# Low rank products of two neighbouring FFN blocks, each on half of TensorE's rows

## What is computed

```python
def _bitlinear(x, w_latent):
    scale = clip(mean(abs(w_latent), axis=1, keepdims=True), 1e-05, None)
    tern = clip(round(w_latent / scale), -1.0, 1.0)
    w = w_latent + stop_gradient(tern - w_latent)
    return x @ (w * scale).T

h = _bitlinear(x, w_fc) + gate * (x @ v.T @ fast_b.T @ u.T)      # hidden 2048, rank 16
r = maximum(h, 0.0)
y = _bitlinear(r * r, w_proj)

x = x + xattn(layernorm(x), ctx, ctx)
x = x + ffn(layernorm(x))
```

## Time and profile before

| | before |
|---|---|
| median of three runs | 2806.88 us |
| span of the profiled execution | 2803.6 us |
| TensorE busy with matmuls | 2666.3 us (95%) |
| VectorE busy | 1688.5 us (60%) |
| ScalarE busy | 1111.7 us (40%) |
| GpSimd busy | 377.6 us (13%) |

### The profile page before, as it was taken

The page is one execution under the profiler, slowest core; times in us unless marked ns, Lnnn a source line. Parts: engine busy times, 40 slices in busy tenths (PEclk is TensorE's granted clock), DMA queues, the critical chain, the costliest instruction groups (busy, mean ns, idle before and its releaser), DMA issues. The chain is left out here.

```text
span 2803.6 us, 46166 instructions
## 1 busy us (share of the span) xinstructions
PE 2666.3 (95%) x15410; PEld 1979.3 (71%) x15410; DVE 1688.5 (60%) x3278; ACT 1111.7 (40%) x1965; POOL 377.6 (13%) x791
## 2 busy tenths in 40 slices
PE   7999999999999999999999967999999999999998
PEld 5666666667666666666766645888888888888887
DVE  4676766776767677677676666444444444444444
ACT  2533443443353344244335245444344334433332
POOL 1212121121121212112112110000000000000000
PEclk9999999999999999999999977999999999999999
DMA  4343253333334325333333332000000000000000
GB/s 129 84 112 99 61 135 92 81 98 98 88 85 114 97 62 134 90 79 103 98 85 88 96 104 76 30 30 30 30 30 30 30 30 30 30 30 30 30 30 31
DMA packets 116803, 198.81 MB, mean 71 GB/s; under 512 B 19987, under 2 KB 22035, under 8 KB 116260
## 3 DMA queue, kind: packets, MB, share of 16 engines
q1 hardware_dynamic: 116772, 198.42, 25.6%
HBM read 63.08 MB, written 33.55 MB: 34 GB/s over the span
## 5 line engine op out<-in xcount | busy, mean ns | idle before, releaser
L715 ACT ACTIVATE probs<-bank 128x512 f32<-128x512 f32 x640 | 369.2, 597 | 339.6 <-PE bank L529 329.6
L1125 PE MATMUL y_bank<-projT,a_hi 128*128 128x512 f32 x1024 | 409.1, 399 | 0.0
L1113 PE MATMUL h_bank<-x2T_hi,fcT 128*128 128x512 f32 x1024 | 406.2, 397 | 0.9 <-ACT scale_row L1196 0.9
L1114 PE MATMUL h_bank<-x2T_lo,fcT 128*128 128x512 f32 x1024 | 406.6, 397 | 0.0
L1127 PE MATMUL y_bank<-projT,a_lo 128*128 128x512 f32 x1024 | 403.9, 394 | 0.0
L1204 ACT ACTIVATE relu<-h_bank,scale_fc 128x512 f32<-128x512 f32 x256 | 176.0, 687 | 464.8 <-PE h_bank L1117 464.8
L464 POOL TENSOR_SCALAR_AFFINE_SELECT probs<-probs 128x256 f32<-128x256 f32 (+1 forms) x640 | 234.1, 366 | 872.7 <-ACT probs L715 870.1
L1314 DVE CAST a_hi<-act_sq 128x512 fp32r<-128x512 f32 x256 | 121.0, 472 | 373.6 <-ACT act_sq L1209 373.6
L529 PE MATMUL bank<-stack 98*128 98x512 f32 (+3 forms) x1024 | 286.0, 351 | 28.3 <-ACT probs L715 26.0
L504 PE MATMUL bank<-stack 96*128 96x512 f32 (+3 forms) x1024 | 266.0, 330 | 17.8 <-DVE maxima L777 11.8
L777 DVE TENSOR_REDUCE maxima<-bank 128x1 f32<-128x512 f32 x256 | 175.9, 687 | 162.2 <-PE bank L508 162.2
(11 more groups left out here) (182 smaller groups left out, 4623.9 us busy)
## 6 DMA issues: line engine op xcount, KB each, us to landing
stack<-stage SPq DMA_DIRECT2D x768, 128.0 KB, 2.3
x_in<-in_x_dram SPq DMA_DIRECT2D x16, 1024.0 KB, 5.3
x<-x_res SPq DMA_DIRECT2D x64, 256.0 KB, 2.4
x_in_sb<-x SPq DMA_DIRECT2D x16, 1024.0 KB, 5.6
out_dram<-y_sb SPq DMA_DIRECT2D x64, 256.0 KB, 2.0
xc_rows<-in_ctx_dram SPq DMA_DIRECT2D x15, 1024.0 KB, 5.2
stack<-m_stage SPq DMA_DIRECT2D x128, 8.0 KB, 1.8
w_nat<-in_L_ffn_w_fc_dram SPq DMA_DIRECT2D x2, 1024.0 KB, 6.7
```

The costliest lines, as they stand in the source:

```text
L715: act.activation(probs[:, s[2], :], t_bank[u % 2][:, :], ACT.Exp, scale=SCALE).then_inc(exp_done, 1)
L1113: pe.matmul(h_bank[b % 2][:, :], fcT[:, k, cols], xT_hi[:, k, :], start=k == 0, stop=False)
L1114: pe.matmul(h_bank[b % 2][:, :], fcT[:, k, cols], xT_lo[:, k, :], start=False, stop=False)
L1125: pe.matmul(y_bank[j][:, :], a_hi[:, b % RING, P * j:P * j + P], projT[:, b, :], start=b == 0, stop=False)
```

## The change

Each pair of blocks b - 1 and b (b odd) has its two low rank products issued one after the other behind the eight large matmuls of block b. The product of the even block takes rows 0 to 63 of `u_stack` and `z_sb`, that of the odd one rows 64 to 127; each writes its own bank and raises `h_full`. For this the four groups of 16 rows are packed into the first 64 rows (at 0, 16, 32 and 48), and stand a second time in the other 64: `a_stack` and `u_cols` are filled accordingly, and the low part of z is made in two operations of 16 rows. The wait for z moves from block 0 to block 1.

```diff
-    assert RANK <= 32 and D == 512 and KT == 4 and HIDDEN_LAG == KT
+    assert RANK == 16 and D == 512 and KT == 4 and HIDDEN_LAG == KT
...
+    HALF = P // 2
...
-                        if b == 0:
+                        if b == 1:
                             pe.wait_ge(xm_free, i * XJ + XJ)
-                        pe.matmul(h_bank[b % 2][:, :], u_stack[:, cols], z_sb[:, :], start=False, stop=True
-                                  ).then_inc(h_full, 1)
+                        if b % 2 == 1:
+                            for m in (b - 1, b):
+                                rows = slice(HALF * (m % 2), HALF * (m % 2) + HALF)
+                                pe.matmul(h_bank[m % 2][:, :], u_stack[rows, P * m:P * m + P], z_sb[rows, :],
+                                          start=False, stop=True).then_inc(h_full, 1)
...
-            for col in (0, 32, 64):
+            for col in (0, 16, 32, 64, 80, 96):
                 last = act.activation(a_stack[:, :, col:col + RANK], a_f32[:, :, :], ACT.Copy)
...
-                    dve.tensor_tensor(z_sb[32:64, :], x_bank[0][32:64, :], z_sb[32:64, :].bitcast(F32), ALU.subtract
-                                      ).then_inc(xm_free, 1)
+                    for at in (32, HALF + 32):
+                        last = dve.tensor_tensor(z_sb[at:at + RANK, :], x_bank[0][at:at + RANK, :],
+                                                 z_sb[at:at + RANK, :].bitcast(F32), ALU.subtract)
+                    last.then_inc(xm_free, 1)
...
-            dve.tensor_tensor(a_stack[:, :, 96:96 + RANK], a_f32[:, :, :], a_stack[:, :, 0:RANK].bitcast(F32),
-                              ALU.subtract).then_inc(prep, 1)
+            for col in (48, 112):
+                last = dve.tensor_tensor(a_stack[:, :, col:col + RANK], a_f32[:, :, :],
+                                         a_stack[:, :, 0:RANK].bitcast(F32), ALU.subtract)
+            last.then_inc(prep, 1)
...
-                    for col, src in ((0, u_hi), (32, u_hi), (64, u_lo), (96, u_hi)):
-                        last = dve.tensor_copy(u_cols[:, :, col:col + RANK], src[:, :, :].bitcast(F32))
+                    for odd in range(2):
+                        for col, src in ((0, u_hi), (16, u_lo), (32, u_hi), (48, u_hi)):
+                            at = HALF * odd + col
+                            last = dve.tensor_copy(u_cols[:, odd::2, at:at + RANK], src[:, odd::2, :].bitcast(F32))
```

## The result

The changed kernel takes 2854.5 us (median of four runs, 2851.3 to 2856.2) against 2806.9 us: a ratio of 1.0168, 95% interval 1.0153 to 1.0182. The forecast was 2857.3 us, in a range from 2834 to 2880, and slower. The profiled execution spans 2849.6 us, 46.0 more than the 2803.6 of before; the forecast for it was 50.4.

The account below looks back on a forecast made before the run. TensorE was taken to bound the FFN, every matmul slot counting. Terms +16.3, +32.6 and +1.5 gave +50.4 us, the span going from 2803.6 to 2854.0; with 3.3 for the median, 2857.3 us, range 2834 to 2880.

Parts of the forecast that it names:

- term 1: FFN pairs: TensorE empties around each, costing 0.17 us instead of saving 0.227; 96 pairs, +16.3 us.
- Rival (a): FFN pairs: no emptying for 64-row halves, loads hide under the last full matmul; 2812.8 us, chance 0.09.
- the assumption behind the 0.44: Within a pair: both halves' loads run together, so the halves start at 0.43 and 0.44 us.
- (b): Within a pair: the two loads follow one another, second half 0.107 us later; +10.3 us, 2867.6, chance 0.10.
- (c): Within a pair: halves run one after the other; 2879.1 us with emptying (chance 0.07), 2834.6 without (0.05).
- (e): FFN pairs: halves stream quicker than a full matmul, without emptying; 2797 us at half a slot, chance 0.03.
- term 2: Batch start: TensorE waits for relu before H2 and H4, +1.02 us each, 32 waits, +32.6 us.
- third wait: Batch start, H3 waiting for relu of block 1: forecast as hidden, relu ending at 2.94 and H2 at 3.59.
- rival (d): Batch starts: the clock falls, up to 1.7 us lost in each of 16 spells, +27; 2884 us, chance 0.05.
- term 3: Setup, run once: added copies, subtraction and z operation lengthen the chain, +1.5 us, between bounds 0 and 2.3.

Follow-up runs that it names:

- pairs_four_banks: Changed kernel with the blocks of h rotating through four PSUM banks instead of two, pairs kept; 2829.6 us.
- half_per_block: Changed kernel, but each block has its own 64-row half product behind its own eight matmuls, no pairs; 2910.4 us.
- quads_four_banks: Changed kernel with four banks, full products except blocks 4 to 11, whose half products stand four at a time behind blocks 7 and 11; 2806.7 us.
- both_on_lower_half: Changed kernel, but the odd block's product also lies on rows 0 to 63, so a pair can't run side by side; 2877.2 us.
- full_deferred: Changed kernel, but both products behind the odd block take all 128 rows instead of halves; 2835.7 us.
- layout_only: Changed kernel's filling and two z operations only; every block has its full product behind its own matmuls, z awaited at block 0; 2814.5 us.

## Why the prediction was right

- *The pair* (term 1) was put at 0.17 us, from the 0.07 at three borders in attention. Measured: 0.165 in pairs_four_banks. The step that carried the sign was to read those borders, of one-row and 128x32 products, as ones of any change of partition; half_per_block shows it for 64 rows, and the 0.07 came back as 0.07 and 0.08. Rival (a), in which the pairs would have saved 21.8 us and only the waits cost, falls with it. The Trainium skill's page "TensorEngine Tiling (Array Packing)", Key Properties, says that a change of tiling mode drains the engine, and the traces here agree: the loads come 0.33 and 0.43 behind the start of the matmul before them, where elsewhere they start with it. The Trainium skill's page "TensorE: Matmul & The Clock Gate", Step-by-step, lets a weight load be pulled ahead of running matmuls into the background buffer; the traces here show that inside one partition only, as with the second pair in quads_four_banks (its loads at 2020.46), and at no change of partition. From how few rows on a product counts as another partition no run settles: 96 rows keep the cover, 64 do not.
- *Both halves together*, the assumption behind the 0.44, held: both start in the same hundredth, and both_on_lower_half prices the other way at 1.37 per batch, or 0.23 for each of the six pairs that no wait follows. Rivals (b) and (c) fall. So does (e): in half_per_block a single half with its load exposed lasts 0.49 and the full matmul behind it, its load exposed too, 0.50; and the second pair in quads_four_banks lasts 0.40 like any full one. Halves stream no quicker.
- *The new waits* (term 2) were put at 1.02 each, two in a batch. Measured: 1.02 at the first pair, 0.85 more than a pair without wait (the changed kernel less pairs_four_banks: 0.85; the wait alone, in full_deferred: 0.84). Two such pairs and six at 0.165 make the 3.03 of a batch. The chain behind them came out step by step: half product to relu 0.42 after the exposed 0.11, relu 0.69, 0.05 to the load. There was no third wait.
- *The clock*: the granted clock is 1.00 over a batch (first line), and 1.00 at a batch start around the first new wait (second line), so rival (d) falls too:

```profile
2060.00:2125.00 65.00, 63.45 (x276) 1.00 0.09 32
2007.00:2010.00 3.00, 2.22 (x10) 1.00 0.22 87
```

  Only the very first matmuls of the loop, which follow the gaps of the setup, stand at the lower of the two levels, 1.2 GHz, in both kernels, before and after:

```profile
1724.70:1728.00 3.30, 3.27 (x8) 0.50 0.65 213
1721.80:1726.00 4.20, 4.20 (x10) 0.50 0.81 246
```

  After the change it is ten matmuls and not eight, 0.43 us apart in place of 0.234. That is 0.4 of the 0.45 us by which the first batch lost more than the others; no run shows why the spell was longer.

- *The setup* (term 3) was put at 1.5. The chain of waits of the changed kernel, to be held against the earlier trace rows:

```profile
1665.85 0.88 ACT a_stack L1171 x6
1666.76 0.36 DVE a_stack L1280 x2
...
1690.39 0.68 DVE z_sb L1262
1691.08 0.70 DVE z_sb L1262
...
1699.87 1.18 DVE u_cols L1300 x8
```

  0.43, 0.70 and 0.27 more, and 0.13 for the second subtraction, which was one of 0.23 before: 1.5 in the parts. From the start of attention's last matmul to that of the loop's first it is 75.8 before and 77.1 after, 1.3 more; in the eight other runs, with the same setup, it is 1.5 to 1.8 more.
- *The sum*. The loop gives 48.9 (forecast 48.9), the setup 1.3, and yet the span grew by 46.0: attention, which the change doesn't touch, ended 4.2 us sooner in this one execution. That the loop agrees to the tenth is in part luck: the pairs cost 0.5 us less than forecast, the first batch 0.45 more. Over the runs the median is 47.6 higher. What was off in the forecast of the median, 2.8 us, is less than the end of attention varies from one profiled execution to another (8 us, below); that attention took it in these four runs is not shown.

## What to carry to other kernels

A matmul on 64 of TensorE's rows is cheap only among its like: going to another partition of the array and back cost about 0.39 us here, as the next load then can't hide under the last matmul, so count the products between two changes, and pair only where the saved slots outweigh it. Before a result is delivered later, ask who takes the buffer next and what stands between; here two banks and no other work for TensorE made a wait of 0.85 us out of a reordering without cost elsewhere. And when a step on a side engine is doubled, look how much its cover had to spare, since 0.1 us was all there was here.

## What the runs showed of the hardware

- Two half products on different rows are as good as one: x2 in 0.51 us with the exposed load, where one takes 0.49 to 0.50. Within one partition they follow each other like full ones, 0.23 apart (0.73 for two on the same rows against 0.50; the second pair of a four).
- A DVE subtraction or addition on 16 rows takes as long as one on 32 or 128 with the same 512 columns: 0.68 to 0.70 (z's low part on 16 rows in layout_only and on 32 before, the residual add on 128), so splitting one by rows doubles it.
- The end of attention, the same code in every kernel here, lay between 1644.7 and 1652.8 us in the profiled executions. The loop behind it repeated to 0.04 us per batch or better within each run. In a kernel like this the distance between two batches tells 0.1 us where the whole time can't tell 3.
